# A four-layer network on one core: layers 2 and 3 with other recurrence products, and inverse masks transposed on VectorE

## What is computed

```python
A0 = tril(-(k_beta @ k.T * L), -1)
A  = solve_triangular(eye - A0, eye)      # inverse of a unit lower triangle
v, k_cumdecay = A @ v, A @ (k_beta * decay_exp)
def step(S, (k_i, v_i, kcd_i)):
    attn  = tril(k_i @ k_i.T * L)
    v_new = v_i - kcd_i @ S
    o_i   = (k_i * de) @ S + attn @ v_new
    S_new = chunk_total_decay * S + (k_i * dw).T @ v_new
out + o @ W_read.T
```

## Time and profile before

| | us |
|---|---|
| median of 3 runs (lowest, highest) | 1829.18 (1828.34, 1829.65) |
| the profiled execution's own time | 1830.12 |
| its span in the trace | 1828.3 |
| TensorE, VectorE, GpSimd, ScalarE busy | 1759.1, 1274.2, 1177.2, 1082.8 |
| mean granted TensorE clock | 0.996 of full |

### The profile page before, as it was taken

The page is one execution under the profiler, slowest core; times in us unless marked ns, Lnnn a source line. Parts: engine busy times, 40 slices in busy tenths (PEclk is TensorE's granted clock), DMA queues, the critical chain, the costliest instruction groups (busy, mean ns, idle before and its releaser), DMA issues.

```text
span 1828.3 us, 31828 instructions
## 1 busy us (share of the span) xinstructions
PE 1759.1 (96%) x10270; PEld 1338.7 (73%) x10270; DVE 1274.2 (70%) x4547; ACT 1082.8 (59%) x2686; POOL 1177.2 (64%) x1547
## 2 busy tenths in 40 slices
PE   7999999999999999999999999999998999999988
PEld 5788988866676666666666676677878887788874
DVE  7863345688869887888889765546557766678684
ACT  5554226566676577777676775456545556544555
POOL 5555658888878877878778863134437664454456
PEclk9999999999999999999999999999999999999999
DMA  6100000010000000000000000000000000000002
GB/s 241 65 25 1 1 3 2 3 48 1 1 2 1 1 1 1 1 1 1 1 1 1 6 5 5 1 1 8 3 1 3 11 21 17 20 2 1 2 9 62
DMA packets 24473, 26.44 MB, mean 14 GB/s; under 512 B 3492, under 2 KB 21284, under 8 KB 23924
## 3 DMA queue, kind: packets, MB, share of 16 engines
q1 hardware_dynamic: 24308, 24.41, 4.1%
HBM read 22.26 MB, written 2.15 MB: 13 GB/s over the span
## 4 chain that ended last, share of the span: by engine, by line
PE 79%; DVE 8%; POOL 6%; ACT 4%; issue 2%; DMA 1%; SPq 0%; POOLq 0%; DVEq 0%; ACTq 0%
PE ps L86 72%; PE ps L89 7%; POOL arena L103 5%; ACT arena L97 4%; DVE arena L103 3%; DVE arena L143 1%; DVE arena L106 1%; DVE arena L109 1%; DVE arena L126 1%; ACT L97 0%; DMA cst<-in_cst 0%; DVE arena L123 0%; DVE arena L129 0%; DVE arena L112 0%; DVE ps L143 0%
## 5 line engine op out<-in xcount | busy, mean ns | idle before, releaser
L103 POOL TENSOR_TENSOR arena<-arena 128x128 f32<-128x128 f32 (+6 forms) x796 | 693.5, 885 | 348.0 <-DVE arena L103 127.5
L97 ACT ACTIVATE arena<-ps 128x128 f32<-128x128 f32 (+13 forms) x1100 | 352.8, 354 | 435.2 <-PE ps L86 312.6
L86 PE MATMUL ps<-arena 128*128 128x128 f32 (+4 forms) x2864 | 460.3, 295 | 18.6 <-DVE arena L103 11.5
L86 PEld LDWEIGHTS ps<-arena 128*128 128x128 f32 x2864 | 381.4, 192 | 118.3 <-issue 63.1
L103 DVE TENSOR_TENSOR arena<-ps,arena 128x128 f32<-128x128 f32 (+4 forms) x696 | 319.1, 470 | 179.4 <-PE ps L86 162.8
L97 ACT ACTIVATE arena<-arena 128x128 f32<-128x128 f32 (+1 forms) x772 | 299.8, 442 | 35.3 <-POOL arena L103 27.5
L97 ACT ACTIVATE arena<-ps,cols 128x512 f32<-128x512 f32 x324 | 218.3, 689 | 170.9 <-PE ps L86 156.0
L86 PE MATMUL ps<-arena,cst 128*128 128x504 f32 (+2 forms) x768 | 289.2, 493 | 8.2 <-POOL arena L103 3.1
L86 PE MATMUL ps<-arena,moe 128*128 128x256 f32 (+1 forms) x960 | 289.7, 441 | 0.6 <-DVE arena L103 0.6
L89 PE MATMUL ps<-cst,arena 128*128 128x128 f32 (+1 forms) x1392 | 238.4, 275 | 14.8 <-ACT arena L97 6.3
L109 DVE SCALAR_TENSOR_TENSOR arena<-ps,arena 128x128 f32<-128x128 f32 (+2 forms) x424 | 141.9, 373 | 131.0 <-PE ps L86 87.1
(11 more groups left out here) (110 smaller groups left out, 1847.6 us busy)
## 6 DMA issues: line engine op xcount, KB each, us to landing
rows<-in_rows SPq DMA_DIRECT2D x1, 2253.0 KB, 15.1
arena<-in_x SPq DMA_DIRECT2D x8, 256.0 KB, 5.0
wf<-in_wf SPq DMA_DIRECT2D x2, 1024.0 KB, 5.9
arena<-in_L_ffn_W SPq DMA_DIRECT2D x8, 256.0 KB, 3.2
out_dram<-arena SPq DMA_DIRECT2D x8, 256.0 KB, 2.8
wmod<-in_wmod SPq DMA_DIRECT2D x4, 384.0 KB, 7.7
arena<-kept SPq DMA_DIRECT2D x24, 64.0 KB, 2.8
arena<-kept SPq DMA_DIRECT2D x8, 192.0 KB, 3.1
```

The costliest lines, as they stand in the source:

```text
L86: return UNSENT if self.e is None else self.e.matmul(out, lhsT, rhs, start=start, stop=stop)
L97: return self.e.activation(out, in_, func, bias=bias, scale=scale)
L103: return UNSENT if self.e is None else self.e.tensor_tensor(out, a, c, op)
```

## The change

Inverse: the input is now built in transposed form directly in `G4`, and for steps 0 to 4 VectorE transposes the 32x32 blocks of G4 (`tr32`) and multiplies by the mask, SBUF to SBUF; steps 5 and 6 stay as they were. Layer 2: W_write and W_read are multiplied together once; c = kT.T @ S; w = vb - gamma*c on VectorE; u = XT.T @ w; vn = beta*u on ScalarE; s = kd.T @ vn; o = gram.T @ vn, and kS, a scaled copy of c, is added to h on GpSimd. Layer 3: c = kT.T @ R, w and u in the same way, the transposes of R and of u in banks of their own; the transposes `e3d` go and GpSimd subtracts the identity from DT. `kd` has two buffers in both layers and is ScalarE's. All four strings of TURNS are new. The core of the diff (PE side, and what it calls):

```diff
+    def tr32(self, out, a):
+        return UNSENT if self.e is None else self.e.transpose(out, a)
...
+            ps = banks.take(pe, b, b, "wwr")
+            pe.mm(ps[:, 0:128], wsm("ww2")[:, 0:128], wsm("wread")).then_inc(*pe.up(b, "wwr"))
...
+        BLOCKWISE = (0,1,2,3,4)
         def inv_pe(b, m, *key):
             for n in range(7):
+                if n not in BLOCKWISE:
+                    ps = banks.take(pe, b, b, "inv_f", n, *key)
                     pe.wait_ge(*at("inv_v", b, n, *key))
+                    for i in range(4):
+                        ins = pe.tr(ps[:, col4(i)], m.G4[:, i, 0:128], ident)
...
         def inv_dve(b, m, *key):
+            for n in range(7):
+                yield
+                if n in BLOCKWISE:
+                    if n:
+                        dve.wait_ge(*at("inv_p", b, n - 1, *key))
+                    dve.wait_ge(*at("inv_v", b, n, *key))
+                    dve.tr32(four(m.Y), m.M4).then_inc(*dve.up(b))
+                    dve.wait_ge(*dve.last(b))
+                    dve.tt(four(m.Y), four(m.Y), over(neg(n)), ALU.mult).then_inc(*dve.up(b, "inv_y", b, n, *key))
...
         def l2_pe(b):
...
-                        pe.wait_ge(*at("d2kb", b, t))
-                        pe.mm(ps[:, 0:128], m.kb, m.XT[:, c]).then_inc(*pe.up(b, "d2c", b, t))
+                        pe.wait_ge(*at("d2S", b, t - 1))
+                        pe.mm(ps[:, 0:128], m.kT[:, c], m.S).then_inc(*pe.up(b, "d2c", b, t))
...
-                    ins = pe.mm(ps[:, 0:128], m.XT[:, c], m.vb[:, c], start=True, stop=(t == 0))
-                        ins = pe.mm(ps[:, 0:128], m.akt, m.S, start=False, stop=True)
+                    pe.mm(ps[:, 0:128], m.XT[:, c], m.w if t else m.vb[:, c]).then_inc(*pe.up(b, "d2u", b, t))
...
+                        pe.mm(ps[:, 0:128], m.kds[t % 2], m.vn).then_inc(*pe.up(b, "d2s", b, t))
...
-                    ins = pe.mm(ps[:, 0:128], m.vn, m.gram[:, c], start=True, stop=(t == 0))
-                        ins = pe.mm(ps[:, 0:128], m.S, m.kTg, start=False, stop=True)
-                        ins = pe.mm(ps[:, 128:256], m.kd, m.vn)
-                    pe.mm(ps[:, 0:128], m.oT, wsm("wread")).then_inc(*pe.up(b, "d2r", b, t))
+                    pe.mm(ps[:, 0:128], m.gram[:, c], m.vn).then_inc(*pe.up(b, "d2o", b, t))
...
         def l3_pe(b):
...
-                    ins = pe.tr(ps[:, col4(i)], m.DT[:, col4(i)], ident)
...
-                        pe.mm(ps[:, 0:128], m.kb, m.XT[:, c]).then_inc(*pe.up(b, "e3c", b, t))
+                        pe.mm(ps[:, 0:128], m.kT[:, c], m.R).then_inc(*pe.up(b, "e3c", b, t))
+                        pe.tr(ps[:, 0:128], m.R, ident).then_inc(*pe.up(b, "e3Rt", b, t))
...
-                    ins = pe.mm(ps[:, 0:128], m.XT[:, c], m.vb[:, c], start=True, stop=(t == 0))
-                        pe.mm(ps[:, 0:128], m.akt, m.R, start=False, stop=True)
+                    pe.mm(ps[:, 0:128], m.XT[:, c], m.w if t else m.vb[:, c]).then_inc(*pe.up(b, "e3u", b, t))
```

More of the change, by code:

```diff
@@ L343, in __init__ @@
             self.h, self.gram, self.S = self.a, r.take(512), r.take(128)
-            self.tri = r.take(512)
-            self.kb, self.kTg, self.akt, self.vn = (self.tri[:, 128 * i:128 * i + 128] for i in range(4))
-            self.kd, self.oT = r.take(128), self.kb
+            spare = r.take(512)
+            self.w, self.vn, self.kS, kd = (spare[:, 128 * i:128 * i + 128] for i in range(4))
+            self.kds = [r.take(128), kd]
             cc = r.take(40)
             self.ss, self.rn, self.nm, self.bt = cc[:, 0:4], cc[:, 4:8], cc[:, 8:12], cc[:, 12:16]
-            self.bg, self.gcol, self.ng, self.dot = cc[:, 16:20], cc[:, 20:21], cc[:, 24:28], cc[:, 36:37]
+            self.gcol, self.ngcol = cc[:, 20:21], cc[:, 21:22]
         else:
@@ L354, in __init__ @@
             self.ss, self.rn, self.bt = cc[:, 0:4], cc[:, 4:8], cc[:, 12:16]
-            self.bg, self.gcols = cc[:, 16:20], cc[:, 20:24]
-            self.arow, self.below, self.tri = G[:, 0:512], self.XT, self.kT
+            self.ngcols = cc[:, 20:24]
+            self.arow, self.above = G[:, 0:512], self.XT
             self.qT, self.gate = self.Y, G[:, 0:512]
-            self.qg, self.u, self.uT, self.kd = (G[:, 128 * i:128 * i + 128] for i in range(4, 8))
-            self.akt, self.sc, self.oT, self.kb = (self.hT[:, 128 * i:128 * i + 128] for i in range(4))
+            self.qg, self.u, self.uT, kd0 = (G[:, 128 * i:128 * i + 128] for i in range(4, 8))
+            kd1, self.sc, self.oT, self.w = (self.hT[:, 128 * i:128 * i + 128] for i in range(4))
+            self.kds = [kd0, kd1]
 class Ffn2:
@@ L382 @@
 TURNS = {
[L383 to L414, removed]
@@ L535, in program @@
         mhalf = sb("mhalf", [128, 8])
-        below = sb("below", [128, 128])[:, :]
+        above = sb("above", [128, 128])[:, :]
         gm = sb("gm", [128, 2])
@@ L1803, in inv_dve @@
         def inv_dve(b, m, *key):
[L1804 to L1807 removed]
+            for n in range(7):
                 yield
[L1809 to L1812 removed]
+                if n in BLOCKWISE:
[5 more added lines that the diff above has]
+                    dve.tt(four(m.Y), four(m.Y), over(neg(n)), ALU.mult).then_inc(*dve.up(b, "inv_y", b, n, *key))
+                else:
+                    ps = banks.get(b, "inv_f", n, *key)
+                    dve.wait_ge(*at("inv_f", b, n, *key))
+                    dve.tt(four(m.Y), four(ps[:, :]), over(neg(n)), ALU.mult).then_inc(
+                        *dve.up(b, "inv_y", b, n, *key, free=(b, "inv_f", n, *key)))
             yield
         def inv_pool(b, m, *key):
+            pool.wait_ge(*at("inv_t", b, *key))
+            pool.tt(m.M4, m.M4, over(ident), ALU.subtract).then_inc(*pool.up(b, "inv_v", b, 0, *key))
+            yield
             for n in range(7):
@@ L1918, in l2_act @@
                 act.wait_ge(*at("d2h", b, g))
-                for i, square in enumerate((m.kd, m.vn, m.akt, m.kTg)):
+                for i, square in enumerate((*m.kds, m.vn, m.kS)):
                     act.act(square, m.h[:, col4(i)], ACT.Square, accum=m.ss[:, i:i + 1]).then_inc(
@@ L2052, in l2_pool @@
                 yield
-                pool.wait_ge(*at("d2tri", b, g))
-                pool.tt(four(m.tri), four(m.tri), over(ident), ALU.subtract).then_inc(
-                    *pool.up(b, "inv_m", b, "l2", g))
-                yield
                 yield from inv_pool(b, m, "l2", g)
@@ L2102, in l3_pe @@
                 yield
-                ps = banks.take(pe, b, b, "e3d", g)
-                for i in range(4):
-                    ins = pe.tr(ps[:, col4(i)], m.DT[:, col4(i)], ident)
-                ins.then_inc(*pe.up(b, "e3d", b, g))
-                yield
                 ps = banks.take(pe, b, b, "e3t", g)
@@ L2272, in l3_dve @@
                 dve.wait_ge(*at("e3g", b, g))
-                dve.cp(m.gcols, ps[:, 0:4]).then_inc(*dve.up(b, free=(b, "e3g", g)))
-                yield
-                ps = banks.get(b, "e3d", g)
-                dve.wait_ge(*at("e3d", b, g))
-                dve.tt(four(m.below), four(ps[:, :]), over(ident), ALU.subtract).then_inc(
-                    *dve.up(b, "e3below", b, g, free=(b, "e3d", g)))
-                yield
-                dve.wait_ge(*dve.last(b))
-                dve.tt(m.bg, m.bt, m.gcols, ALU.mult).then_inc(*dve.up(b))
+                dve.ts(m.ngcols, ps[:, 0:4], -1.0, None, ALU.mult).then_inc(*dve.up(b, free=(b, "e3g", g)))
                 yield
@@ L2359, in l3_pool @@
                 rsqrt_pool(b, m.rn, m.ss, 1e-24, ALU.max, "e3ss", b, g)
-                yield
-                pool.wait_ge(*at("e3tri", b, g))
-                pool.tt(four(m.tri), four(m.tri), over(ident), ALU.subtract).then_inc(
-                    *pool.up(b, "inv_m", b, "l3", g))
+                pool.wait_ge(*at("e3scan", b, g))
+                pool.tt(four(m.above), four(m.DT), over(ident), ALU.subtract).then_inc(*pool.up(b, "e3above", b, g))
                 yield
```

397 lines of the change are left out of this document (198 added, 199 removed).

## The result

The changed kernel takes 1770.78 us (median of 4 runs, 1767.42 to 1773.78) against 1829.41 us; the ratio is 0.968, 95% interval 0.9662 to 0.9698. The forecast was 1769 us, range 1750 to 1802. The total is right; two of its terms are not, by amounts that cancel, and most of what follows is about them. The profiled execution took 1771.47 us, its span is 1769.7 us.

A forecast was written before the change was run, and what follows sets the result against it. The prediction took layers 2 and 3 as mostly bound by TensorE's throughput: 64.4 us of work removed, less 8 us new idle, plus 4 us returning, is 60.4 us, so 1769 us; range 1750 to 1802.

The forecast's parts named there:

- Prices and counts: Whole change: 353 transposes at 0.110 us and 230 matmul records fewer on TensorE; VectorE's blockwise transpose at 0.70 us.
- the 64.4 us: TensorE work removed: 37.0 us in layer 2, 27.3 us in layer 3, 0.1 us for the mask.
- The term for new idle time: Layers 2 and 3: 8 us of new TensorE idle charged, 4 us of idle ahead of removed transposes credited.
- both stages are mostly bound by TensorE's throughput: Layers 2 and 3: TensorE busy 272.3 of 282 and 248.2 of 258 us, with a few per cent of chain waits.
- Rival E: Every stage's order is rewritten: idle could move some 10 us; extreme, 60 us lost elsewhere, about 1829 us, chance 0.03.
- The sum: Whole kernel: 64.4 - 8 + 4 = 60.4 us saved, giving a median of 1769 us.
- signs of being wrong: Transpose over 1.2 us, over 10 us of multiply waits, VectorE over 90% in layer 3, or gain before 1225 us.
- sign of 10 us of waits for VectorE's multiply: The forecast would be wrong if TensorE waited for VectorE's multiply by more than 10 us in all.
- Rival B: Removed TensorE records also give busy time back: 93 us, 1737 us; halfway, about 1752 us; chance 0.15.
- Rival C: VectorE becomes the bound in layers 2 and 3 with the blockwise transpose at 1.85 us: 1802 us; chance 0.10.
- Rival D: TensorE's written order waits for late blockwise transposes, 80 times the delay; at 1.85 us 1861 us; chance 0.03.
- F: A TensorE transpose's price is its duration, 0.277 us: 98 us in place of 39, 1710 us; chance 0.02.

The follow-up runs named there:

- dead_tr: Changed kernel with TensorE again doing the four transposes of each blockwise inverse step as dead work nobody waits for: 1785.24 us, ratio 0.9751.
- dead_mm: Changed kernel with 112 of the 116 matmuls the recurrences lost put back as dead work before the waits for w and vn: 1780.98 us, ratio 0.9733.
- both splices: Orders swapped up to each element's layer 2 entry: changed code with the old early order, 1825.3 us; the code before with the new early order, 1814.25 us.
- tr32_twice: Changed kernel with each blockwise VectorE transpose done twice in a row ahead of its mask: 1814.18 us, ratio 0.9916.
- no_tr32: Changed kernel without its 80 blockwise transposes, the mask multiplied with the untransposed block, every wait kept: 1763.1 us, ratio 0.9637.
- act_halves: Changed kernel with ScalarE writing the new half of an inverse's odd and even columns, masked, from PSUM, GpSimd multiplying only the old half: 1770.22 us, ratio 0.9672.

## Why the prediction came out right, and where it was wrong

- **Prices and counts: right.** 9687 records, 0.705 us for the transpose, VectorE's share of layer 2 is 193.4 of 273.9 us, 71% (75% forecast), of layer 3 205.0 of 259.5 us, 79% (83% forecast), its dense stretch 84%; both are lower because the stages got less short than forecast. TensorE's busy time fell by 64.6 us; that this meets the 64.4 us is chance, since 18.6 of them fell ahead of layer 2, where almost no work was removed, and 45.9 behind its entry.
- **The term for new idle time: wrong, and the main failure.** I took 8 us of new idle against 4 us coming back. The part from layer 2 on gained 21.0 us for 64.4 us of work, so 43 us did not come back: 25.0 us are idle time by name, the other 18 lie in busy time that fell by less than the work, through groups that overlap less and the lower clock, which no run here tells apart. Dead work in these places costs 41% of its price (dead_tr, dead_mm). The step that failed is the one from "TensorE is busy 96 to 97%" to "both stages are mostly bound by TensorE's throughput". It held beside the experts (4.5 us for 5.4 in dead_tr) and not in the two stretches with attention alone, where 50 us of the work were removed and 8.8 us came back. The busy share was read from modelled busy times and from an order made for that load; it doesn't say that TensorE would stay filled with an eighth less work.
- **Rival E, the rewritten order: mis-sized.** I allowed +-10 us; the order up to layer 2 alone is worth 37.6 us in the changed kernel and 40 us in both splices. It was visible as a possibility (24.8 us idle in 350 to 1050 us; after, 326 to 983 us has 8.0), and I took a quarter of its size. Even the idle time would not have bounded it: up to the entry it fell by 19.0 us (39.7 to 20.7), the other 18.6 are busy time, with the same work.
- **The sum: right by chance.** 43 us lost where 4 net were charged, 38 gained where none was counted. The prediction named its own signs of being wrong, and one of them came: the gain lies before 1225 us, for 37.6 of 58.6 us. The layers were to become 37 and 27 us shorter and became some 8 and 10.5. Its sign of 10 us of waits for VectorE's multiply can't be read by itself: the waits of TensorE's matmuls for all of VectorE's two-operand work are 14.5 us, where they were 16.6.
- **Rival B** (busy time comes back too) is refuted in its direction: removed records come back at under their price by starts, not over it. **Rival C**'s price never came (0.705 us). **Rival D**'s mechanism is real: tr32_twice adds 0.74 us per step (two transposes and the mask behind them start 1.48 us apart, one and its mask 0.74) and costs 43 us, 0.54 us per step, the clock's part among it; at the measured price it had no excess to work on. **F** fell with the counts.
- **The cause of the waits.** Beside the experts TensorE is the bound: it is busy 138.2 of 138.7 us, and dead work there costs nearly its price. In the attention-only stretches no engine is. Adding dead TensorE work costs 2.2 us for 12.2 and 6.1 us for 15.2; over the whole kernel, relieving VectorE gives back 14% (no_tr32), relieving GpSimd nothing, moving VectorE's work to ScalarE nothing, while adding to VectorE costs 37% off the chain and 77% in it, all with the clock's share in them. Every engine keeps a written order, and each waits for the next piece in it. That the order itself holds the time is an argument from this pattern; a newly searched order for one of the relieved kernels, which would show it, was not tried. No tried version beats the changed kernel with the same computation.

## What to carry to other kernels

Price removed work by starts, but then ask of each stage whether anything else is ready to run in the hole: put dead work of the removed size back where it stood, and read what it costs stage by stage. It says whether that engine binds there; it is not the worth of a removal, since what is added and what is taken away count differently in a written order. A change that brings a new order for the whole program is two changes; splice the orders and compare the time at a common point, stage by stage, before crediting the arithmetic. In a program with written orders a relief tested without a new order shows a lower bound.

## What the runs showed of the hardware that I had not expected

TensorE's granted clock differs between kernels in the same part of the work, and how much TensorE idles doesn't settle it. In layer 2's attention-only stretch it is 1.00 before (TensorE 130.7 of 140.4 us busy), 0.96 after (111.8 of 135.2) and 0.91 in tr32_twice:

```profile
1327.80:1479.10 151.30, 119.60 (x788) 102.39 (x788) 120.56 (x327) 74.74 (x246) 100.38 (x197) 0.91 0.04 10
```

A mean of 0.91 is 2 x 0.09 x 151.3 = 27 us at the lower of the two levels. But act_halves keeps 1.00 in the same part, where its TensorE is idle as much as the changed kernel's:

```profile
1326.00:1461.00 135.00, 112.06 (x809) 95.05 (x808) 103.10 (x311) 85.48 (x291) 95.81 (x200) 1.00 0.05 12
```

and no_tr32 has 0.99 with TensorE busy 108.7 of 132.2 us. What decides it these runs don't show. A kernel can be steady in it: 0.985 or 0.986 over the whole kernel in all 4 runs of tr32_twice. It goes with the spread of the runs: after, 1767.42 us came with a granted 0.997 and 1773.78 us with 0.993. The kernel before varies in the same way on other chips, 1827.79 us at 0.998 to 1832.35 us at 0.993.
